# One-core Mamba-2 block and ternary FFN: the MLP of tile i-1 laid between the chunk steps of tile i

## The reference, cut to what matters

```python
x = x + attn(x); x = layernorm(x)            # N = 4096 rows of 256
x = layernorm(x + ffn(x))
# attn:
zxbcdt = rmsnorm(x) @ w_in                   # 256 -> 1288: z 512, xbc 768, dt 8
xc = silu(conv4(xbc) + conv_b)               # -> xh (8 heads of 64), B, C (128 each)
dt = softplus(dt_raw + dt_bias); a = -dt * exp(a_log); u = dt * xh
y = chunked_scan(a, B, C, u) + d_skip * xh   # decay matrix, diagonal part, state part
h = x + (rmsnorm(y * silu(z)) * norm_w) @ w_out
m = square(relu(rmsnorm(h) @ w_fc)) @ w_proj # the MLP: 256 -> 1024 -> 256
return h + m
# ffn: ternary weights, 256 -> 1024 (gated) -> 1024 -> 1024 -> 256, scales per channel
```

## Time and profile before

| | us |
|---|---|
| median of 3 runs (1417.06 to 1417.64) | 1417.12 |
| the profiled execution | 1419.12 |
| its span, first to last instruction | 1417.4 |
| from the start to the chunk stage of tile 0 | 52.8 |
| one tile of part A, from its sums of `a` to the next one's | 88.7 to 88.9 |
| part B with the last layer norm, from 749 us on | 668 |

### The profile page before, as it was taken

The page is one execution under the profiler, slowest core; times in us unless marked ns, Lnnn a source line. Parts: engine busy times, 40 slices in busy tenths (PEclk is TensorE's granted clock), DMA queues, the critical chain, the costliest instruction groups (busy, mean ns, idle before and its releaser), DMA issues. The chain is left out here.

```text
span 1417.4 us, 19529 instructions
## 1 busy us (share of the span) xinstructions
PE 1294.2 (91%) x6546; PEld 1059.7 (75%) x6546; DVE 804.5 (57%) x1432; ACT 633.1 (45%) x1206; POOL 254.6 (18%) x215
## 2 busy tenths in 40 slices
PE   5599898998989989889778999999999999999996
PEld 3477686776867768677566888888888888888886
DVE  6776776767767677676724245262624436262543
ACT  5457475474754747547354132242414223141410
POOL 4414325143151431514310000000000000000000
PEclk9799898998989989899898999999999999999998
DMA  3220020200202002020207000000000000000000
GB/s 127 97 82 16 15 82 15 96 15 15 81 15 96 15 15 81 15 96 0 89 1 300 0 1 30 0 30 0 15 15 0 30 0 30 0 30 0 1 15 16
DMA packets 23645, 55.89 MB, mean 39 GB/s; under 512 B 2368, under 2 KB 20416, under 8 KB 20928
## 3 DMA queue, kind: packets, MB, share of 16 engines
q1 hardware_dynamic: 23616, 55.50, 10.7%
HBM read 35.57 MB, written 19.92 MB: 39 GB/s over the span
## 5 line engine op out<-in xcount | busy, mean ns | idle before, releaser
L1357 ACT ACTIVATE full<-bank,scale 128x512 f32<-128x512 f32 x128 | 88.3, 690 | 384.0 <-PE bank L1260 384.0
L1260 PE MATMUL bank<-hB_lo,h_sb 128*128 128x512 f32 x512 | 200.2, 391 | 0.0
L1260 PE MATMUL bank<-hB_hi,h_sb 128*128 128x512 f32 x512 | 199.7, 390 | 0.0
L1260 PE MATMUL bank<-hA_hi,h_sb 128*128 128x512 f32 x512 | 199.2, 389 | 0.0
L1260 PE MATMUL bank<-hA_lo,h_sb 128*128 128x512 f32 x512 | 199.2, 389 | 0.0
L1422 DVE CAST hA_hi<-full 128x512 fp32r<-128x512 f32 x64 | 27.3, 427 | 185.9 <-ACT full L1357 185.9
L1371 POOL TENSOR_TENSOR rsv_b<-mv_b,eps 128x4 f32<-128x4 f32 x8 | 10.7, 1341 | 656.0 <-DVE mv_b L160 656.0
L485 PEld LDWEIGHTS bank<-u,E 128*128 128x128 f32 x512 | 82.0, 248 | 57.4 <-issue 47.7
L930 DVE SCALAR_TENSOR_TENSOR xc<-xp,conv_w_sb,xc 128x512 f32<-128x512 f32 x144 | 121.7, 892 | 1.5
L485 PE MATMUL bank<-u,E 128*128 128x64 f32 x512 | 84.1, 335 | 36.5 <-DVE E L979 36.5
L1260 PEld LDWEIGHTS bank<-hA_lo,h_sb 128*128 128x128 f32 x512 | 96.1, 188 | 20.1
(11 more groups left out here) (208 smaller groups left out, 3089.4 us busy)
## 6 DMA issues: line engine op xcount, KB each, us to landing
chk<-w_ffn SPq DMA_DIRECT2D x8, 1408.0 KB, 5.8
ffn_raw<-chk SPq DMA_DIRECT2D x8, 1408.0 KB, 4.8
h_sb<-ffn_raw SPq DMA_DIRECT2D x2, 4096.0 KB, 17.7
x_in<-x SPq DMA_DIRECT2D x8, 512.0 KB, 3.8
x_rows<-x SPq DMA_DIRECT2D x8, 512.0 KB, 3.0
x_in<-x_rows SPq DMA_DIRECT2D x8, 512.0 KB, 4.5
out<-o_sb SPq DMA_DIRECT2D x8, 512.0 KB, 3.2
xp<-w_in SPq DMA_DIRECT2D x1, 1288.0 KB, 6.8
```

Of the source, the lines that this page charges most:

```text
L1260: ins = pe.matmul(o, a_, b_, start=first and n == 0, stop=last and n == 1, skip_group_check=True)
L1357: nc.scalar.activation(full[:, n % FULL, :], b[:], ACT.Gelu, scale=scale[:, 1 + n // KH, n % KH:n % KH + 1]).then_inc(s_gd, 1)
```

## The change

Part A becomes: `turn_h` and the MLP of tile i-1 stand in the chunk stage of tile i; the front stage of tile i+1 stands alone. Tiles 0 and 1 are written out (tile 0 has no MLP in it, tile 1 no normalization of an earlier `x1`), a loop runs tiles 2 to 6, tile 7 is written out, and behind it stands a tail with the MLP of tile 7. The tables give the places: two `fc` behind `pre(0)`, then in step c up to one `proj` (in step 3 two) and one `fc` ahead of `main(c)`, and one of each behind it. The scores and the transposed B leave their bank by one ScalarE copy into `GB`, so that `gb` is an item of ScalarE's two banks now, and VectorE multiplies from SBUF. The low parts of even j are GpSimd's, those of odd j VectorE's. `h_rms` moves from the end of the MLP to step 0. The residual `x` is loaded a second time from DRAM into `x_res`, in place of the copy `keep_x`. The weight piece goes to `ffn_raw` by a DMA from DRAM to DRAM, and `chk` holds half a piece, loaded twice in a tile. The sums for the decay operands (`cum`) go through a VectorE bank instead of bank5.

```diff
+TURN_XN = CH - 2
+Z_FIRST = 1
+START_FC = (0, 1)
+STEP_FC = ((2, 3), (4, 5), (6, 7), ())
+STEP_PROJ = (((), (0,)), ((1,), (2,)), ((3,), (4,)), ((5, 6), (7,)))
...
@@ PE
-                def iteration(w, i, more):
+                def iteration(w, i, before, more):
+                    mlp = before is not None
+                    if mlp:
+                        turn_h(w, before)
                     sums_of_a(w, i)
                     pre(w, i, 0)
+                    for j in START_FC if mlp else ():
+                        fc(w, j)
                     for c in range(CH):
+                        early_fc, late_fc = step_fc(c) if mlp else ((), ())
+                        early_proj, late_proj = STEP_PROJ[c] if mlp else ((), ())
                         if c < CH - 1:
                             pre(w, i, c + 1)
+                        for j in early_proj:
+                            proj(i - 1, j)
+                        for j in early_fc:
+                            fc(w, j)
                         if c > 0:
                             turn_y(w, i, c - 1)
                         main(w, i, c)
+                        for j in late_proj:
+                            proj(i - 1, j)
+                        for j in late_fc:
+                            fc(w, j)
                         if c > 0:
                             out_rows(w, i, c - 1)
...
-                    turn_h(w, i)
-                    for j in range(KH):
-                        fc(w, i, j)
-                        if j > 1:
-                            proj(w, i, j - 2)
-                        if more and j < CH:
-                            z_rows(w, j)
...
@@ ACT
+                    b = item(w, f"gb{c}")
...
+                    nc.scalar.activation(GB[:, c % 2, :], b[:, 0:2 * P], ACT.Copy).then_inc(s_ad, 1)
...
                     for c in range(CH):
                         if c < CH - 1:
                             pre(w, i, c + 1)
+                        for j in early_fc:
+                            fc(w, i - 1, j)
                         if c > 0:
                             yT(w, c - 1)
                             gate_rms(step, w, i, c - 1)
                             low_sum(i, c - 1)
+                        if mlp and c == 0:
+                            h_rms(i - 1, before)
+                        for j in late_fc:
+                            fc(w, i - 1, j)
                         if more and c == 1:
                             x_rms(step, i + 1)
...
@@ POOL
+                        if mlp:
+                            m_lo_part(i - 1, 2 * c)
                         pool.wait_ge(s_sup, CH * i + c + 1)
@@ DVE
-                        if c < CH - 1:
-                            pre(w, i, c + 1)
...
                         main(step, w, i, c)
+                        if mlp:
+                            m_lo_part(i - 1, 2 * c + 1)
+                        if c < CH - 1:
+                            scores(w, i, c + 1)
...
+                    if mlp:
+                        sum_x1(i - 1)
                     yT(w, CH - 1)
```

More of the change, by code:

```diff
@@ new lines, with step_fc, pre_items, act_items @@
+assert len(STEP_FC) == CH and KH == 8
+def step_fc(c):
+    return STEP_FC[c][:1], STEP_FC[c][1:]
+F_ACT = ["dt"] + [f"xbc{m}" for m in CONV_ORDER] + [f"z{c}" for c in range(CH)]
+F_DVE = ["yT3", "wo3"]
+def pre_items(c):
+    return [f"{n}{c}" for n in ("xt", "gb", "dlo", "dhi")]
+def act_items(mlp, more):
+    order = ["cums"] + pre_items(0) + [f"fc{j}" for j in START_FC if mlp]
+    for c in range(CH):
+        order += pre_items(c + 1) if c < CH - 1 else []
+        order += [f"fc{j}" for j in STEP_FC[c] if mlp]
+    return order + (F_ACT if more else [])
@@ new lines, in dve_items, with hi_items, orders @@
+def dve_items(mlp, more):
+    order = ["hT0", "hT1"] if mlp else []
+    for c in range(CH):
+        order += ([f"yT{c - 1}"] if c > 0 else []) + [f"yoff{c}", f"ydiag{c}"] + ([f"wo{c - 1}"] if c > 0 else [])
+        order += ["xnT0", "xnT1"] if more and c == TURN_XN else []
+    return order + F_DVE + (["cum"] if more else [])
+def hi_items(order):
+    return [n for n in order if "T" in n]
+def orders(act, dve):
+    return act, dve, hi_items(dve)
+M_ACT = [f"fc{j}" for j in range(KH)]
+M_DVE = ["hT0", "hT1"]
@@ L83, with __init__ @@
 class Where:
-    def __init__(self, orders, i):
+    def __init__(self, orders, i, before):
         self.orders = orders
-        self.base = [0 if orders is FIRST else len(f) + len(o) * i for f, o in zip(FIRST, LOOP)]
-        self.first = [0 if orders is FIRST else len(f) for f in FIRST]
+        self.first = [sum(len(o[n]) for o in before) for n in range(3)]
+        self.base = [f + len(o) * i for f, o in zip(self.first, orders)]
     def act(self, name):
@@ L1091, in iteration @@
                     add_out(w, i, CH - 1)
[L1092 to L1093 removed]
                     if more:
                         taps(step, w, i + 1, (5,))
+                        dt_and_a(step, i + 1)
                         taps(step, w, i + 1, (0, 1))
[L1097 removed]
                         taps(step, w, i + 1, (2, 3))
                         halo(i + 1)
[L1100 to L1110 removed]
+                        sums_lo(w, i + 1)
                     assert step.n == (per if more else CM_STEPS), step.n
@@ L1148, in _ @@
                 halo(0)
-                sums_lo(0)
-                keep_x(0)
+                sums_lo(w, 0)
                 assert step.n == F_STEPS
-                iteration(Where(LOOP, 0), 0, True, first=True)
-                with dve.Fori(1, TILES - 1) as i:
-                    iteration(Where(LOOP, i), i, True)
-                iteration(Where(LAST, TILES - 1), TILES - 1, False)
+                iteration(w_first, 0, None, True, False)
+                iteration(w_loop(1), 1, w_first, True, False)
+                with dve.Fori(2, TILES - 1) as i:
+                    iteration(w_loop(i), i, w_loop(i - 1), True, True)
+                iteration(w_last, TILES - 1, w_loop(TILES - 2), False, True)
+                hT(w_tail)
+                x_plus_h(TILES - 1, w_last)
+                norm_x1(TILES - 2)
+                scale_x1(TILES - 2)
+                for j in range(1, KH, 2):
+                    m_lo_part(TILES - 1, j)
+                sum_x1(TILES - 1)
+                norm_x1(TILES - 1)
+                scale_x1(TILES - 1)
         a_ctx.close()
```

383 lines of the change are left out of this document (201 added, 182 removed).

## The result

The changed kernel takes 1485.57 us (median of 4 runs, 1481.13 to 1488.46), the kernel before beside it 1417.38 (1417.06 to 1417.85, 4 runs). The ratio is 1.0478, with a 95% interval of 1.0452 to 1.0504: 4.8% slower. The direction and the mechanism were forecast; the time lies 40.6 us above the predicted 1445, and 1.6 us above the range's end.

A forecast was written before the change was run, and what follows sets the result against it. TensorE bounds the front stage and MLP, a chain over engines the chunk stage. Tile 0 -20.0, tiles 1 to 6 +25.1, tile 7 +23.8, tail -1.4: +27.5 on 1417.1 gives 1445 us, range 1392 to 1484.

The forecast's parts named there:

- The rival with this mechanism: Clock falls in the chunk stage: 5.9 us at 1.2 GHz after two waits 1472, after three 1493; chance 0.18.
- F: Front stage alone, first dt product to next dlo0: VectorE bounds it, 26.4 us, TensorE idle about 8 us.
- start of C: Chunk stage from dlo0 to the end of ydiag(0): 13.05 us at full clock, 14.7 with first products at 1.2 GHz.
- step 0 to 1: Chunk stage link between the first two steps, through VectorE's low part, ScalarE's fc and xt, then TensorE: 14.0 us.
- step 1 to 2: Chunk stage, ydiag(1) to ydiag(2): the 14.0 us step plus x_rms 2.7 us between fc and xt, 16.7 us.
- step 2 to 3: Chunk stage, ydiag(2) to ydiag(3), with no pre: 12.0 us.
- end: Chunk stage after ydiag(3): y(3), state masking, low part of 7, proj(7), wo(2), 7.2 us; TensorE idles 3.5 ahead of proj(7).
- C: Chunk stage with the MLP in it: links sum to 64.6 us, plus 1 us clock for each of two waits, 66.5.
- The link over VectorE, the low part at 4.4 us behind `ydiag`: Chunk steps: VectorE's odd low part, behind y, ends 4.4 us after ydiag, 3.5 if it need not wait for GpSimd.
- I take 1 us for each: Chunk stage: half clock behind two TensorE waits (4 and 3.5 us) costs 1 us each, at most 2.95 possible.
- Tile 0's chunk stage stays at 33.4: Tile 0 has no MLP, so its chunk stage stays at 33.4 us; the next dlo0 comes 20.0 us earlier.
- Scores shut out by GpSimd: Rival: VectorE's scores, read from GB, held by GpSimd, 0.9 us in three steps of seven tiles: 1464; chance 0.07.

The follow-up runs named there:

- e10: Changed kernel with proj(6) and proj(7) moved behind the front stage's last z block and sum_x1 behind the low sums: 1422.82 us, ratio 1.0037.
- e5: e3 with proj(6) and proj(7) moved into the front stage and sum_x1 behind the low sums: 1363.14 us, ratio 0.9611.
- e2: Changed kernel with VectorE making the odd low parts at the top of its step, ahead of the sums of y: 1410.09 us, ratio 0.9945.
- e1: Changed kernel with ScalarE running x_rms ahead of fc(5) in step 1 instead of behind it: 1460.01 us, ratio 1.0306.
- e3: Changed kernel with both reorderings, x_rms ahead of fc(5) and odd low parts at the top of VectorE's step: 1388.21 us, ratio 0.9792.
- b1: Kernel before with the scores through GB, cum in a VectorE bank and the weight check in halves, MLP not moved: 1419.90 us, ratio 1.0012.
- b2: Kernel before with the weight check in halves alone: 1417.73 us, ratio 0.9996.
- e7: Changed kernel with useless matmuls, 24 ahead of chunk 3's score product and 34 around chunk 0's xt transposes: 1467.66 us, ratio 1.0340.
- e4: Changed kernel with 24 useless matmuls ahead of chunk 3's score product: 1471.25 us, ratio 1.0378.
- e6: e3 with 34 useless matmuls around the chunk stage's first transposes, 20 ahead and 14 behind: 1377.22 us, ratio 0.9714.

## Why the prediction was wrong, by its own steps

The direction was right, and so was the chain. The number was not: the clock beyond the start was priced at 2 us a tile and costs 6.0, two links were walked 1.9 us short, and tile 0 took 5 us more than was counted. The rival with this mechanism had 0.18, its two-wait case 1472 and its three-wait case 1493. That the time lies between is in part luck: the rival took 3 us for each stretch where 1.6 to 2.3 were measured, and the short links and tile 0 made up for it.

| step | predicted | measured, tile 3 |
|---|---|---|
| F | 26.4 | 26.9 |
| start of C | 14.7 | 14.6 |
| step 0 to 1 | 14.0 | 15.3 |
| step 1 to 2 | 16.7 | 19.9 (17.7 at full clock) |
| step 2 to 3 | 12.0 | 12.8 (12.9) |
| end | 7.2 | 9.6 (7.3) |
| clock, beyond the start | 2 | 6.0 (1.6, 2.1 and 2.3), in the rows above |
| C | 66.5 | 72.1 |
| tile 0, dlo0 to dlo0 | 59.8 | 64.8 |

- *F, VectorE bounds it: right.* e10 shows it, as 2.8 us more of TensorE's work don't lengthen F. That TensorE idles for about 8 us was too much: it is 26.9 - 21.6 = 5.3 us, nearly all in three waits ahead of the first `dlo`, of which `from_s` releases only the last, 0.80 us. The sum of 17.7 us left out `turn_h`, the sums of `a` and the transposes of `pre(0)`, some 3 us; in e5, at full clock, TensorE is busy for 23.55 - 2.8 = 20.8.
- *The link over VectorE, the low part at 4.4 us behind `ydiag`: right.* The state product starts at 328.97, the low part ends at 333.24. What the earlier trace rows showed of `low_bits` holds for the low part: in steps 0 to 2 of tiles 1 to 7 it takes 1.53 us each time, beside GpSimd's decay of the state, and in step 3, without it, 0.69. In e2, where it stands elsewhere, its median is 0.69.
- *`x_rms` on the chain, 2.7 us: right*, by e1.
- *"I take 1 us for each" of two waits: the step that failed.* I argued that 5.9 us at half clock cost at most 2.95 of progress and often none, and took a third of that. But behind both long waits TensorE's work is the limit, and nothing hides it: 2.1 and 2.3 us. The end is the plain case: proj(7) and wo(2) take 2.7 and 2.6 us instead of 1.4 each, and the link 9.6 against 7.3. The first link had such a stretch too (335.90 to 339.30), which costs 1.6, though its waits are 1.26 us; I had counted only waits of over 3 us. The row of the kernel before held a warning: 42.5 us at a mean clock of 0.80 are 2 x 0.20 x 42.5 = 17 us at the lower level, and I took from it one stretch of 5.9. The changed kernel's stage has 20.9.
- *Steps 1 to 2 and 2 to 3 at full clock: 1.0 and 0.9 us short.* In both the low part comes later than walked. In step 1 it ends at 349.99, 5.7 us behind the start of the state product at 344.25, where 4.4 were taken: VectorE begins the gating later, behind `yT`'s low part, and `tmp<-tmp,y` and `y<-tmp,z_s` take 0.98 and 1.18 us instead of 0.69 beside GpSimd's `y` and its even low part. In step 2 VectorE's `xn` (1.92 us) stands ahead of the sums of `y`; the low part ends 370.90 - 364.12 = 6.8 us behind the state product, where 6.0 were counted, and TensorE waits 0.66 us for it. No run changes either by itself.
- *Tile 0's chunk stage stays at 33.4: wrong*, it took 38.2. `yT(2)` waits 2.92 us for `h` at 81.24, as VectorE now does the scores of chunk 3 ahead of `add_out(1)`, and TensorE runs at half clock from 79.9 for 10.2 us. Not all of the 4.8 us are the edit's: with the same instructions the stage took 35.7, 35.6, 38.6 and 35.7 us in e1, e2, e3 and e10, with 7.8, 7.7, 14.2 and 7.8 us at the lower clock against 13.6 here. It is the place where an edit that I costed at nothing showed in the profile; b1 says that over all tiles the scores' new way costs nothing to be measured.
- *Halves and `GB`: nothing, right*, by b1 and b2. The second load of `x` was not tried alone.
- *Scores shut out by GpSimd: not where a low part stands ahead of them*; there `E<-E,GB` takes 1.21 us (349.91). Tile 0 has no low part, and its three scores behind `main` each meet the decay of the state. The third is on the way to `h`, for which TensorE waits 2.92 us; 0.85 us of that wait are this hold (2.06 against 1.21). The rival was priced for tiles 1 to 7, and in tile 0 it came true:

```profile
78.72 2.06 DVE L1074 TENSOR_TENSOR E<-E,GB 128x1024 f32<-128x1024 f32 x1
...
78.28 1.43 POOL L965 TENSOR_TENSOR S<-S,dec 128x512 f32<-128x512 f32 x1 [3.27 <-DVE S L1090]
...
81.24 1.11 PE L555 MATMUL bank<-ident,y 128*128 128x128 f32 x4 [2.92 <-DVE h L1111]
```

In e2 no score has a low part ahead of it, and 24 of 32 take 2.1 us, as this one:

```profile
323.76 2.06 DVE L1074 TENSOR_TENSOR E<-E,GB 128x1024 f32<-128x1024 f32 x1
```

That is what the Trainium skill, "SBUF — State Buffer", section "Who interferes with whom", says of a VectorE instruction with two SBUF inputs; the trace agrees, and the 0.85 us are of the size that the prediction gave such a hold (0.9).

Of the signs named ahead, those of the waits came true: `dlo` of chunk 3 waits longest, for `xt`, and the Relu and `proj(7)` wait for `m_lo`. Those of size did not: the clock is 0.86 (below 0.85 was named), a tile takes 98.8 us (92 to 93), and TensorE idles for 5.3 us ahead of the first `dlo` (7 to 9).

The sum: tile 0 gave back 15.0 us where 20.0 were counted; six tiles cost 6 x (98.8 - 88.7) = 60.7 where 25.1 were; tile 7 and the rest 776.3 - 752.5 = 23.8 where 22.4 were. In all 69.5 against 27.5 in profiled executions. Of the 42 us between them the mis-sized clock is the largest part, about 24; the short links are some 10, F 3, tile 0 5 and tile 7 1.4. The turning point of C = 62.6 was about right: e10, with C at 62.2 to 64.2 and F at 25.6, ends 0.4% over the kernel before.

## What to carry to other kernels

When work is laid between the links of a chain, look at each engine's own order before counting busy time: the same instructions took 1485.6 or 1388.2 us, and what differed was whether a 0.7 us subtraction and a 2.7 us statistic stood ahead of or behind the instruction that another engine waited for. Put what is ready early first, and put work into the stage whose bound is another engine (the front stage took 2.8 us of products for nothing). And price a wait of TensorE by itself and by the work at half clock behind it, at its full size whenever TensorE's products are what comes next on the chain. How much of that work there is, the stage before the change shows better than the length of one wait.

## What the runs showed of the hardware

**The same waits, with and without the lower clock behind them.** In e10, which runs one loop body for both tiles, TensorE waits 1.43 us and then 0.16 or 0.17 ahead of the first decay product. In one tile that product takes 0.50 us, in the next 0.79:

```profile
293.82 0.33 PE L517 MATMUL bank<-ident,xc 128*128 128x128 f32 x1 [1.43 <-ACT dec L808]
...
294.54 0.50 PE L525 MATMUL bank<-to_l,from_s 128*128 128x512 f32 x1 [0.16 <-POOL from_s L933]
...
381.69 0.33 PE L517 MATMUL bank<-ident,xc 128*128 128x128 f32 x1 [1.43 <-ACT dec L808]
...
382.42 0.79 PE L525 MATMUL bank<-to_l,from_s 128*128 128x512 f32 x1 [0.17 <-POOL from_s L933]
```

Their chunk stages are 62.2 us at a clock of 0.95 and 64.1 at 0.90. The wait of 3.21 us ahead of `proj(7)` shows it too: in the changed kernel 6.8 us at the lower clock go with it in tile 3, in e7 none in tile 3 and 3.4 us in tiles 2, 4, 5 and 6. What decides between them, no run separates. So waits of equal length are not followed by equal clock, and a forecast of the clock from the waits alone has an error of about 2 us a tile here. The Trainium skill, "TensorE: Matmul & The Clock Gate", section "Part 1: The HAM clock gate (the "warmup" mystery)", says that the number of matmuls at the lower clock, counted from a kernel's start, varies from run to run of one kernel. The traces here agree in that they show it from tile to tile, and in tile 0's stage from one kernel to another with the same instructions.

**Work without use can pay.** 24 matmuls whose product is overwritten made the changed kernel 14.3 us faster (e4), 34 made e3 11.0 us faster (e6). Real work in the same wait paid more: e5 is 14.1 us faster than e6.
